# The first y^T of a two-layer cross-attention through TensorE's transposes, v(0) in the bank of row sums, and a prologue in another order

## What is computed

```
# layer 0, softmax over the keys
Q = x Wq + bq;  K = c Wk + bk;  V = c Wv + bv
x1 = x + softmax_keys(Q K^T / sqrt(512)) V Wo + bo
# layer 1, softmax over the QUERIES (axis 1), then layer norm
q = x1 Wq' + bq';  k = c Wk' + bk';  v' = c Wv' + bv'
w = softmax_queries(q k^T / sqrt(512))
out = layernorm(w v' + x1) * gamma + beta
```

## Time and profile before

| what | value |
|---|---|
| runs, us | 1167.65, 1169.9, 1170.25 (median 1169.9) |
| the profiled execution, us | 1168.34 |
| its span, first to last instruction, us | 1166.6 |
| around the span, us | 1.7 |
| granted TensorE clock, mean | 0.998 |
| busy, us: PE, DVE, ScalarE, GpSimd | 1144.0, 901.7, 856.0, 961.9 |
| DMA, 5 to 10, 10 to 15, 15 to 20 us, GB/s | 362, 421, 428 |
| IN (1 MB), median us from issue to landing | 4.9 |

### The profile page before, as it was taken

One profiled execution on the slowest core, in us unless ns is written; L12 is line 12 of the kernel. 1 busy time (PEld: TensorE's weight loads), 2 busy tenths in 40 slices (PEclk: granted clock), 3 DMA queues, 4 the chain that ended last, 5 costly groups with the idle time before them and its releaser, 6 DMA issues.

```text
span 1166.6 us, 25294 instructions
## 1 busy us (share of the span) xinstructions
PE 1144.0 (98%) x7980; PEld 1065.8 (91%) x7980; DVE 901.7 (77%) x2085; ACT 856.0 (73%) x1733; POOL 961.9 (82%) x768
## 2 busy tenths in 40 slices
PE   9989999999999999999999999999999999999995
PEld 7789999999999999999999999999999999999984
DVE  5667777777778778778778778777777777777877
ACT  3557777777777777777777777777777777777763
POOL 3458898898888888889889889889889889888865
PEclk9999999999999999999999999999999999999999
DMA  8665676766666666666666666667666667666541
GB/s 314 200 215 176 223 238 198 229 234 194 227 225 215 221 222 216 216 220 220 221 214 222 221 212 229 211 216 236 200 223 230 203 229 233 199 224 233 167 140 74
DMA packets 131695, 249.04 MB, mean 213 GB/s; under 512 B 15696, under 2 KB 88912, under 8 KB 123344
## 3 DMA queue, kind: packets, MB, share of 16 engines
q1 hardware_dynamic: 130656, 247.59, 64.1%
q10 hardware_dynamic: 1008, 1.06, 0.3%
HBM read 165.16 MB, written 83.43 MB: 213 GB/s over the span
## 4 chain that ended last, share of the span: by engine, by line
PE 94%; DVE 1%; POOL 1%; ACT 1%; DMA 1%; issue 1%; SPq 0%; DVEq 0%; ACTq 0%; POOLq 0%
PE bank L378 90%; PE bank L456 2%; PE bank L518 1%; PE bank L544 1%; PE bank L525 0%; DMA yT_raw<-y_dram 0%; DMA gT<-g_dram 0%; SPq L266 0%; POOL Y L1459 0%; DVE y_blk L1008 0%; POOL Y L1473 0%; POOL Y L1476 0%; DVE stats L1084 0%; POOL yT_lo L1402 0%; DMA y_dram<-y_blk 0%
## 5 line engine op out<-in xcount | busy, mean ns | idle before, releaser
L1402 POOL TENSOR_TENSOR xT_lo<-IN,xT_hi 128x1024 fp32r<-128x1024 f32 (+1 forms) x64 | 154.0, 2407 | 25.6 <-ACT xT_hi L667 25.6
L1402 POOL TENSOR_TENSOR yT_lo<-yT_raw,yT_hi 128x1024 fp32r<-128x1024 f32 x63 | 149.9, 2380 | 16.8 <-ACT yT_hi L667 15.5
L1473 POOL TENSOR_TENSOR Y<-Y,gamma_b 128x512 f32<-128x512 f32 x124 | 157.9, 1297 | 1.9 <-ACT Y L803 1.9
L1476 POOL TENSOR_TENSOR Y<-Y,beta_b 128x512 f32<-128x512 f32 x124 | 158.4, 1300 | 0.0
L803 ACT ACTIVATE Y<-R,nmr,rstd 128x512 f32<-128x512 f32 x126 | 96.0, 809 | 72.5 <-POOL nmr L1450 72.5
L378 PE MATMUL bank<-yT_hi,A_hi 128*128 128x256 f32 x512 | 144.5, 282 | 2.7 <-issue 2.7
L378 PE MATMUL bank<-xT_hi,A_hi 128*128 128x256 f32 x512 | 144.8, 283 | 1.1 <-DVE A_lo L1178 1.1
L378 PE MATMUL bank<-xT_hi,A_lo 128*128 128x256 f32 x512 | 144.4, 282 | 0.0
L378 PE MATMUL bank<-yT_lo,A_hi 128*128 128x256 f32 x512 | 144.2, 282 | 0.0
L378 PE MATMUL bank<-xT_lo,A_hi 128*128 128x256 f32 x512 | 144.0, 281 | 0.0
L1448 POOL TENSOR_TENSOR rstd<-ve,half 128x2 f32<-128x2 f32 x63 | 44.1, 700 | 120.9 <-DVE nmu L1099 120.9
(11 more groups left out here) (139 smaller groups left out, 4241.1 us busy)
## 6 DMA issues: line engine op xcount, KB each, us to landing
IN<-in_packed SPq DMA_DIRECT2D x63, 1024.0 KB, 4.9
R<-in_x SPq DMA_DIRECT2D x64, 512.0 KB, 4.3
y_dram<-y_blk SPq DMA_DIRECT2D x252, 128.0 KB, 2.6
yT_raw<-y_dram SPq DMA_DIRECT2D x63, 512.0 KB, 3.6
out<-Y SPq DMA_DIRECT2D x63, 512.0 KB, 2.6
E_dram<-E_blk SPq DMA_DIRECT2D x256, 64.0 KB, 1.8
PT_raw<-E_dram SPq DMA_DIRECT2D x64, 256.0 KB, 2.8
gT<-g_dram SPq DMA_DIRECT2D x64, 128.0 KB, 3.8
```

What stands on the lines that cost most here:

```text
L1402: return nc.gpsimd.tensor_tensor(dst, src, fp(hi), ALU.subtract)
L1473: nc.gpsimd.tensor_tensor(y[:, q, :], y[:, q, :], gamma_b[:, :], ALU.mult).then_inc(Y_mul, 1)
L1476: last = nc.gpsimd.tensor_tensor(y[:, q, :], y[:, q, :], beta_b[:, :], ALU.add)
```

## The change

Sequence 0's y^T is no longer written to DRAM and read back. PE transposes R[0], four 128x128 pieces for each half q, into two banks: the bank of row sums (half 0) and the bank of second scores (half 1). ScalarE copies them out as the high part, DVE subtracts for the low part. v(0) goes into the bank of row sums instead of bank 1; Pc(2) therefore waits for PcT_lo(1) and not for v_lo(0). One matmul of 512 columns (ones by Bv) writes all of the second scores' bank ahead of v(0), and the seed of S1(0) waits for it (`flags_set`) instead of for A1_lo. The DRAM counters of y are one sequence lower (`back=1`). The prologue lists of all five engines are reordered. body and tail have the same steps in the same order.

```
+    def first(self, of=0):
+        return self.base is None and self.k == of
...
+        def v_in(n):
+            return s_bank if n.first() else v_bank
+        yT_first_bank = (s_bank, S1_bank)
... SP, prologue
+            weights(WvT0_s, WvT0, wv0_in)
             load_c0()
             weights(Wo0_s, Wo0, wo0_in)
-            weights(WvT0_s, WvT0, wv0_in)
...
             write_E0(Seq(1))
+            read_E0(Seq(1))
             load_IN(Seq(4))
-            read_E0(Seq(1))
-            write_y(Seq(0))
-            read_y(Seq(0))
             write_E0(Seq(2))
             read_E0(Seq(2))
             write_g(Seq(0))
             write_y(Seq(1))
             read_g(Seq(0))
             read_y(Seq(1))
... PE
-                first(pe, v_lo, n.count(back=2))
+                if n.first(2):
+                    pe.wait_ge(Pc_lo, n.count(back=1))
+                else:
+                    first(pe, v_lo, n.count(back=2))
...
+            def yT_first(q):
+                if q == 0:
+                    pe.wait_ge(ident_set, 1)
+                    pe.wait_ge(c1_set, 1)
+                else:
+                    pe.wait_ge(A1_lo, 1)
+                pe.wait_ge(x1_set, Seq(0).count(2, q))
+                for d in range(DT):
+                    last = nc.tensor.transpose(yT_first_bank[q][:, d * P:(d + 1) * P], R[0][:, q, d * P:(d + 1) * P],
+                                               ident[:, :])
+                last.then_inc(yT_first_full, 1)
             def v_first():
                 pe.wait_ge(A1_lo, 2)
+                pe.wait_ge(yT_lo, 1)
+                nc.tensor.matmul(S1_bank[:, :], ones[:, :], Bv[0][:, 0, :], start=True, stop=True).then_inc(flags_set, 1)
                 v_(Seq(0))
...
             out_first()
+            S0_(Seq(2))
             g1_product()
-            S0_(Seq(2))
             u_(Seq(3))
             Pc_(Seq(1))
+            yT_first(0)
+            yT_first(1)
             out_(Seq(1), 0)
             out_(Seq(1), 1)
             v_first()
... ScalarE, prologue: the new order in full
             xT_h(0) A0_h(0) A0_h(1) cT_h(0) u_h(0) C_h(0) xT_h(1) Bv_h(0) exps0(0) C_h(1) Bv_h(1) cT_h(1)
             u_h(1) xT_h(2) cT_h(2) A1_h(0) PT_h(0) out_seed(0) exps0(1) V1_h Pc_h(0) C_h(2) A1_h(1) u_h(2)
             xT_h(3) cT_h(3) C_h(3) out_seed(1) PT_h(1) u_h(3) Pc_h(1) exps0(2) yT_first_h out_seed(2)
             PT_h(2) v_h(0) S1_seed_first
... DVE, prologue: the new order from u_l(0) on
             u_l(0) c1_parts max0(0) Bv_l(0) E0_blocks(0) Bv_l(1) c1_ u_l(1) g1_parts max0(1) A1_l(0)
             E0_blocks(1) Pc_l(0) V1_l u_l(2) A1_l(1) x1(0,0) x1(0,1) max0(2) g1_ u_l(3) Pc_l(1) E0_blocks(2)
             dots_first g_blocks(0) x1(1,0) x1(1,1) yT_first_l y_blocks(1) v_l(0)
... GpSimd, prologue: the new order in full
             xT_l(0) cT_l(0) C_l(0) xT_l(1) cT_l(1) C_l(1) xT_l(2) PT_l(0) identity cT_l(2) xT_l(3) PT_l(1)
             C_l(2) PT_l(2) C_l(3) cT_l(3)
```

More of the change, by code:

```diff
@@ L430, in v_ @@
                 pe.wait_ge(yT_lo, n.count())
-                if n.plus(1).there():
+                if n.plus(1).there() and not n.first():
                     pe.wait_ge(Pc_lo, n.plus(1).count())
-                else:
+                elif not n.first():
                     pe.wait_ge(v_lo, n.count(back=1))
                 for l in range(LT):
-                    last = product(cols(v_bank, l), lambda a, t: A1[a][:, t, l * P:(l + 1) * P],
+                    last = product(cols(v_in(n), l), lambda a, t: A1[a][:, t, l * P:(l + 1) * P],
                                    lambda b, t: by_q(yT[b], t), DT)
@@ L856, in _ @@
             Bv_h(0)
+            exps0(Seq(0))
             C_h(Seq(1))
             Bv_h(1)
-            exps0(Seq(0))
             cT_h(Seq(1))
             u_h(Seq(1))
+            xT_h(Seq(2))
+            cT_h(Seq(2))
+            A1_h(0)
+            PT_h(Seq(0))
             out_seed_first()
[L863 to L866, removed]
             exps0(Seq(1))
```

76 lines of the change are left out of this document (45 added, 31 removed).

## The result

The changed kernel takes 1167.06 us (median of 14 runs, 1166.42 to 1167.68); the kernel before, beside it on the same chip, takes 1169.89 (14 runs, 1167.65 to 1170.5). The ratio is 0.9979 [0.9972, 0.9986]: faster by 0.21%, just beyond the bound within which the prediction called it "the same".

What follows compares the result with a forecast made beforehand. The prediction took the start of S1(0), waiting for its seed behind the read of gT, as the bound. A 0.66 us gain gave 1167.7 on the profiled execution and 1169.3 on the median; forecast 1168.5, range 1165.8 to 1170.6.

Steps and rivals of the forecast that it cites:

- the same: Whole kernel: a time within 0.2%, 2.3 us, of the kernel before; chance 0.81.
- the 0.66: Ahead of S1(0): y_blk(1) starts at 59.15, not 59.81, so the gT read and S1(0) come 0.66 us earlier.
- Then x1(1,1), 0.71, ends at about 57.9: DVE after out(1,1) ends at 57.13: x1(1,1) takes 0.71, then the subtractions end at about 59.1 and y_blk(1) follows.
- (a): Ahead of S1(0): the read of gT lands late, in 4.5 us, 0.5 slower than before, 1168.9; chance 0.12.
- (c): SP's queue: load_IN(4), waiting for C_lo(2), holds later reads and writes; 1170.9 if C_lo(2) comes at 58; chance 0.05.
- (d): After Pc(1): the transposes run one after the other, 0.8 later than forecast, 1168.5; chance 0.05.
- (b): At S1(0): the seed does not bind, S1(0) starts at 64.3, gain capped at 1.5, 1166.9; chance 0.08.
- (b2): PE's waits up to S1(0): all four vanish, less 1.4 added, 5.2 gained, 1163.1; chance 0.04.
- cT_h(0), now behind A0_h, has 6 us until S0(0): nothing.: Start of the kernel, ScalarE: moving cT_h(0) behind A0_h costs nothing, since S0(0) comes 6 us later.
- From there on PE never waits until the tail: After S1(0) at 67.08: no PE wait until the tail, so a gain at 67 us comes through whole.
- That execution lies 1.56 below the median: Basis of the sum: 0.66 off the profiled 1168.34 gives 1167.7, on the median of runs 1169.3; middle 1168.5.

Runs made afterwards that it cites:

- transposes_one_line: The kernel before with y(0)'s transposes, v(0) in the row sums' bank and the flags matmul, old lists except cT_hi(0) behind both A0_hi: 1167.13 us, ratio 0.9987.
- order_only: The kernel before with the new order of the engine lists, y(0) still going through DRAM: 1169.28 us, ratio 1.0003.
- early_g: The changed kernel with the dots, write and read of gT moved ahead of the y(1) writes: 1166.08 us, ratio 0.9977 to the kernel before.
- after_again: The changed kernel with no edit, measured again for a second profile: 1166.49 us, ratio 0.998 to the kernel before.
- one_line: The kernel before with one ScalarE line moved, cT_h(0) behind the two A0_h: 1167.49 us, ratio 0.9988.
- after_c_first: The changed kernel with cT_h(0) put back ahead of the two A0_h on ScalarE: 1171.16 us, ratio 1.0018 to the kernel before.
- pe_code: The kernel before with cT_h(0) behind the A0_h, plus nine unused matmuls behind Pc(1), y(0) still through DRAM: 1167.15 us, ratio 0.9981.
- before_again: The kernel before with no edit, measured again for a second profile: 1169.27 us, ratio 1.0.
- transposes_old_order: The changed kernel with all engine lists back in the old order, except that the identity is made early: 1168.33 us, ratio 0.9991 to the kernel before.
- spare_trip: The changed kernel plus an unused DRAM round trip of y(0)'s size ahead of load_IN(4): 1167.51 us, ratio 0.9992 to the kernel before.

## Why the prediction came out as it did

**The steps up to S1(0) held.** Forecast and measured: eight transposes overlapping, 1.04 in all, at 52.66 and 52.50; out(1) 54.07 and 54.08; v(0) 59.5 and 59.58; y_blk(1) 59.15 and 59.26; read_g 62.24 and 62.35; S1(0) 66.42 and 66.42; the waits ahead of it about 4.5 and 4.7. But the prediction gave the 0.66 to the end of the DRAM trip alone. Its line "Then x1(1,1), 0.71, ends at about 57.9" takes for granted that DVE is free when out(1,1) ends, and that is so only because g1_ and g_blocks(0) have moved forward: transposes_one_line, without that, starts y_blk(1) hardly sooner than the kernels with y(0) in DRAM, and order_only, without the transposes, no sooner at all. The step needs both. early_g confirms from the other side that the seed is what bound. Beside after_again, whose out(1) starts at the same 53.21, S1(0) came 1.6 us earlier there and the span became 1.5 shorter; v(1) kept the rest.

**The rivals.** (a), (c) and (d) did not come in the changed kernel: gT landed in 3.22, load_IN(4) left at 50.96, the transposes overlapped. (b) and (b2) needed the seed out of the way, which the change doesn't do; (b)'s 1166.9 lies close to the measured 1167.06, but by another mechanism. That the time lies inside the range says little for the sum, since the range is 4.8 us wide.

**What failed is the size of the sum.** The term was 0.66 and the medians give 2.8. Three places of the prediction are behind this:

1. "cT_h(0), now behind A0_h, has 6 us until S0(0): nothing." It asked only who waits for cT_h(0), and not what cT_h(0) holds up. ScalarE stood in front of it until c0 landed, and both A0_h stood behind it, which u(0) needs. The line is worth 1.64 by the medians of one_line. out(1) starts at 54.07, 55.17 and 55.34 in the profiles with cT_h(0) in front (after_c_first, 58.36, left out) and between 53.07 and 54.08 in those with it behind.
2. "From there on PE never waits until the tail" is true, but the tail was left out of the sum: the change was said to move the end only "by moving the start of S1(0), or by making a later product wait", and not by ending a wait. There was a wait in the tail for the last P^T, of 0.3 to 1.0 us from profile to profile of the kernels with y(0) in DRAM, and mostly one of 0.6 behind it, that the other kernels haven't got. The trace that the prediction read had 0.29 of it, and it was not costed.
3. The sum was made against one execution of 1168.34, 1.5 below the median. It happened to be one in which W0 and c0 landed so that the wait for A_lo was 1.07. "That execution lies 1.56 below the median" was in the text, and the right question, what the other executions do in place of it, wasn't asked.

**The account, by medians.** one_line and after_again ran beside the same kernel before. The line takes 1169.13 to 1167.49, which is 1.64; the rest of the change takes 1167.49 to 1166.49, which is 1.00. Of that 1.00 the term at S1(0) is 0.66 by the prediction's sum, and 0.34 is left for the tail. Together 2.64, near the 2.8 of the first measurement. The intervals (about 1 us wide each way) allow each term to be some tenths larger or smaller, and one pair speaks against a tail term in the medians: transposes_one_line and pe_code ran on one chip and took 1167.13 and 1167.15, though the profile of pe_code has a wait of 0.46 in the tail and the other has none.

**By profiles** the division is another. Take the span less the start of out(1), which leaves out the start. With y(0) in DRAM it is 1112.5, 1113.5, 1114.0, 1113.0 and 1112.3 (before, its second profile, order_only, one_line, pe_code; mean 1113.1), in the changed kernel 1111.4 and 1111.2: 1.8 gained behind out(1), of which 0.66 up to S1(0) and 1.1 in the tail. The table has it profile by profile (us; the waits of the tail are PE's for PT_lo and ahead of the transposes):

| profile | y_blk(1) less out(1) | S1(0) less out(1) | waits of the tail | span less S1(0) |
|---|---|---|---|---|
| before | 5.74 | 13.01 | 0.29 | 1099.5 |
| before_again | 5.69 | 12.92 | 0.84, 0.61 | 1100.6 |
| order_only | 5.82 | 13.21 | 0.99, 0.55 | 1100.8 |
| one_line | 5.55 | 12.54 | 0.58, 0.59 | 1100.4 |
| pe_code | 5.71 | 12.68 | 0.46 | 1099.6 |
| transposes_one_line | 5.64 | 12.56 | none | 1099.0 |
| after | 5.18 | 12.34 | none | 1099.1 |
| after_again | 5.17 | 12.08 | none | 1099.1 |

The second column moves by more than the first, since the read of gT lands in 2.97 to 3.38 us. The start gives 1.0 (out(1) at 54.6, the mean of the two profiles of before, and at 53.6, that of after's two). The sum is again 2.8. The profiled executions of one_line and pe_code took 1.1 and 0.8 more than their medians, so the tail's wait in them is probably not that of every execution; the medians have more runs, and I give them the word on sizes.

What is shown: the line on ScalarE, by doing it alone and by undoing it; the earlier y_blk(1), by the chain of the profile, step for step, and that it takes the transposes and DVE's order together, by the two kernels that have one of them. The tail's waits are shown to be there or not; in the profiles they are worth 0.3 to 1.5, in the medians 0.3 or nothing, and their cause is not shown. In the pair order_only and transposes_old_order neither half gained: the first has the regular start but pays for load_IN(4) and in the tail, and the second has the old start and the old order on DVE.

## What to carry to other kernels

When a step is moved in the list of an engine that works in order, ask not only who waits for it but what stands behind it while it waits, above all where it waits for a load. Look at a second profile of the same kernel before forecasting a fraction of a per cent: where the profiled execution lies away from the median, find the stage in which executions differ, since a change that makes it regular gains what no single profile shows. Before giving a gain to one part of a change, ask which other part the sum takes for granted. And read the waits of the tail too before saying that nothing behind a point can move.

## What the runs showed of the hardware

- PE's granted clock fell after a wait of 1.56 to 3.63 us at the start of the kernel, and u(0) took 4.59 to 5.49 us for 3.12. Near 60 us, behind PE work that had run dense for 25 us and more, it stayed at 1.00 after waits of 2.48 to 2.95 us in eight profiles and fell after 2.60 in one (transposes_old_order, 0.50 from 62 to 64 us). After the same wait of 2.13 it stayed in two profiles and fell in two (spare_trip, 0.50 from 60 to 62, and after_c_first, 0.50 from 64 to 66).
- Eight fp32 transposes of 128x128 take 1.04 us, where each lasts 0.27: they overlap as matmuls do.
- A DVE instruction on SBUF alone lasted as long as GpSimd's beside it. In the second profile of before, DVE's and GpSimd's timeline at 1130 us:

```profile
1130.14 2.39 DVE L1098 TENSOR_SCALAR ve<-mv 128x2 f32<-128x2 f32 x1
```

```profile
1130.11 2.40 POOL L1402 TENSOR_TENSOR yT_lo<-yT_raw,yT_hi 128x1024 fp32r<-128x1024 f32 x1 [1.12 <-ACT yT_hi L667]
```

The 128x2 operation takes 0.17 otherwise; here, and in the same place in order_only (2.32), it ended with GpSimd's. PE's last transposes waited 0.6 for DVE in both, but in one_line too, where the operation took 0.17, so that this wait isn't explained by it alone. In the changed kernel one term of g1_parts, of 128x512, took 2.38 beside xT_lo(2); in the kernel before it took 0.48 with GpSimd idle. The Trainium skill (GPSIMD Engine Reference, 1. Specifications) says that GpSimd and VectorE share their way to SBUF and get in each other's way for some kinds of VectorE instructions. The trace agrees: in these three places the DVE instruction was held until GpSimd's ended.
